# Sums of four heads in two packed attentions: one piece of eight products, or two halves in neighbouring steps

## The chip, the cores and the metric

The kernel runs on one core of a Trainium2 chip. The metric is the device time of one execution in microseconds. TensorE (PE in the profile) multiplies matrices, VectorE (DVE), ScalarE (ACT) and GpSimd (POOL) work element by element, and SyncE (SP) issues the transfers. Each engine works through its own list of instructions in order, and semaphores tie the lists together.

## What is computed

The reference is a chain of four attention layers on 16 sequences of 128 rows by 256 numbers. Layers 0 and 2 are ordinary transformer layers. Layers 1 and 3 are the ones that matter here: attentions with 16 heads of only 8 channels each, over 256 positions ("units" are its two halves of 128). Layer 1 needs for each head the mean and the spread of the values, layer 3 a plain attention. Cut to the core:

```python
# layer 1
attn = softmax(einsum('bhqd,bhdk->bhqk', q * scale, k))
mean = einsum('bhqk,bhkd->bhqd', attn, v)
ex2 = einsum('bhqk,bhkd->bhqd', attn, v * v)
std = sqrt(relu(ex2 - mean * mean))
# layer 3
attn = einsum('bhqd,bhkd->bhqk', Q, K) / math.sqrt(DH)
ctx = einsum('bhqk,bhkd->bhqd', softmax(attn), V)
y = ctx @ Wo
```

## The kernel before

The stages run one after the other: layer 0 to about 1270 us of the span, layer 1, layer 2 from about 1600 us, layer 3 from about 2184 us, and its feed-forward to the end. Both packed attentions are made by the same function, `attention(third, ...)`, with `third` 0 for layer 1 ("attention 1" from here on) and 1 for layer 3 ("attention 3"). A window is one batch, 16 windows run the core, and each window has 16 steps `j`, one for each head. The order of the instructions on every engine is written out by hand, step by step, and pieces of neighbouring batches are mixed into one window: `core` is batch n itself, `following` the next one, `carry` the one before, `ahead`, `coming` and `fourth` later ones.

In every step PE makes, for head j of this batch, two products of shifted scores (line 925) and, for head j of the next batch, two products of plain scores (line 934). Both use 32 rows of the array (form 32*128); the text calls the four a pair. DVE takes the maxima of the plain scores (line 1725), ACT the exponential of the shifted ones (line 1405) into `probs_t`. Shifted scores have two banks, so the pair of step j waits until the exponential of step j-2 is done.

Four heads make a pack. When the exponentials of a pack are there, PE sums them with the values (line 984): for each unit c and each of the four heads m one product of form 128*32, each with 32 columns of its own, all into `sum_bank`, half of bank 5. A product of plain floats appears as two instructions, so a pack is 16 instructions. They stand in steps 3, 7, 11 and 15; those of step 3 are the last pack of the batch before. ACT copies the bank out one step later (line 1362), at the head of its steps 0, 4, 8 and 12.

The other half of bank 5 is `spare`. PE turns the maxima there (line 905, steps 1 and 9), DVE copies them out at the head of its steps 2 and 10 (line 1706), and SP moves the copies into rows of q by four transfers (line 2331), which the shifted scores of steps 0 and 8 wait for. In attention 3 PE also turns the heads there (line 1053, step 13), ACT copies them (line 1389, step 14), and the output product (line 1061, step 15) takes that copy. As both halves are in one bank, the sums wait for each of these copies, and these turns wait for the copy of the sums.

Other pieces of a window: projections of q and k (lines 953 and 960; q in step 2, k in step 2 or 3), placing of q and k for later heads (line 912; in attention 1 in steps 0, 11 and 14, in attention 3 in steps 0, 1, 10 and 11; ACT and DVE copy them out, k for the first heads by line 1738), the turn of the summed heads (line 999, steps 6 and 7), the values (line 1010, step 9), in attention 1 the result (line 1022, step 12), whose copies by ACT (lines 1384 and 1385) free the bank that k's placing of step 14 takes. Attention 3 prepares later batches as well: DVE aggregates statistics in step 5 (line 1986), POOL makes the inverse roots from them (lines 2196 to 2202) and the normed rows (line 2206), and PE turns these in step 13 (line 1037), followed by the turn of the placed rows (line 1046). Where two pieces share a step, they stand in the order of the code, in which the sums come behind the scores, projections and the turn of maxima, and ahead of the placings of `place_q_first` and `place_k_first`, the turns of lines 999 to 1053 and the result.

```python
SCHEDULE1 = Schedule(place_k=0, project_k=2, turn=(6, 7), values=9, place_q_first=11, place_k_first=14, result=12)
SCHEDULE3 = Schedule(place_k=1, project_k=3, turn=(6, 7), values=9, place_q_first=11, place_k_first=10, result=15)
TURN_MAXIMA = (9, 1)
LAST_SUMS = 3
```

Of the kernel before, what the change touches and what calls it, by code (L numbers as in the profile page):

```python
# [29 lines left out]
D = 256  # L30
# [20 lines left out]
HN = 16  # L51
# [8 lines left out]
PACK = 4  # L60
# [162 lines left out]
LAST_SUMS = 3  # L223
STD_PARTS = 4
# [188 lines left out]
def program(nc, t, out, outer):  # L413
# [303 lines left out]
    def _(pe):  # L717
# [173 lines left out]
        def attention(third, w_q, source_q, w_k, w_v, when):  # L891
# [5 lines left out]
            def window(n, at, u=None):  # L897
# [18 lines left out]
                for j in range(HN):  # L916
# [51 lines left out]
                    if j % PACK == LAST_SUMS and (j > LAST_SUMS and core or j == LAST_SUMS and carry):  # L968

                        g = (j // PACK - 1) % PACKS  # L970
                        v = vn[u] if j > LAST_SUMS else vn[1 - u]
                        if g == 0:
                            pe.wait_ge(s.v_taken if third else s.v_ready, n + 1)
                        pe.wait_ge(s.exp_ready, HN * n + j - 3)
                        after(pe, s.sums_copied, PACKS * n + j // PACK - 1)
                        if j == LAST_SUMS:
                            pe.wait_ge(s.max_copied, 2 * n + (2 if core else 0))
                        if j == TURN_MAXIMA[0] + 2 and following:
                            pe.wait_ge(s.max_copied, 2 * (n + 1) + 1)
                        if j == HN - 1 and third and carry:  # L980
                            pe.wait_ge(s.heads_copied, i)
                        for c in range(UNITS):
                            for m in range(PACK):
                                last = pe.matmul(sum_bank[quad[m], :], v[:, c, PACK * g + m, :],  # L984
                                                 probs_t[(PACK * g + m) % 8][:, c * D:(c + 1) * D], start=c == 0, stop=c == UNITS - 1)
                        last.then_inc(s.sums, 1)
# [61 lines left out]
                    if third and carry and j == 13:  # L1048
                        pe.wait_ge(s.heads_taken, heads_taken(1, n))
                        if core:  # L1050
                            pe.wait_ge(s.sums_copied, PACKS * n + 2)
                        for unit in range(UNITS):
                            last = pe.transpose(spare[:, unit * P:(unit + 1) * P], heads_out[unit][:, 0:P], ident[:, :])
                        last.then_inc(s.heads_turned, 1)
# [175 lines left out]
    def _(act):  # L1230
# [107 lines left out]
        def attention(third, q_bias, k_bias, when):  # L1338
# [11 lines left out]
            def window(n, at, u=None):  # L1350
# [3 lines left out]
                for j in range(HN):  # L1354
# [32 lines left out]
                    if third and carry and j == 14:  # L1387
# [1030 lines left out]
```

## Time and profile before

| | us |
|---|---|
| median of 3 runs | 2591.17 (2588.92 to 2597.12) |
| the profiled execution, its own time | 2597.26 |
| its span, first to last instruction | 2595.5 |
| mean granted clock of TensorE | 0.932 of full |

PE is busy for 2261.8 us, DVE for 1783.5, ACT for 1481.9 and POOL for 718.5. Times in the timelines are microseconds from the start of the span: the start of a row, how long it lasts, the engine, the line, what is written and read, the shape, and how many neighbouring instructions the row merges. In brackets stands how long the engine was idle just before and what released it. A matmul's duration includes its way through the array, so neighbours overlap, and the distance between starts tells what one holds PE for. In a view of a narrow window only the instructions still running in it are merged.

### The profile page before, as it was taken

The page shows a single profiled execution, that of the slowest core. Times are in us where ns is not written, and L with a number is a line of the kernel's source. Part 1 is how long each engine was busy: PE and PEld are TensorE (multiplying, and loading weights), DVE is VectorE, ACT ScalarE, POOL GpSimd, SP SyncE. Part 2 cuts the span into 40 slices and gives each one's busy share as a digit, 9 for nine tenths or more (in the row PEclk, how much of TensorE's full clock was granted, in tenths as well). Part 3 has the DMA queues.
Part 4 walks back from the last instruction along what each step waited for, and adds up shares of the span by engine and source line. Part 5 has one row for each costly group of instructions (what it writes and reads, how often), then busy time and mean ns, then how long its engine had stood idle before and what let it go on. Part 6 is the DMA issues. An engine that isn't in the chain of part 4 may idle for free. (4 is left out here: it accounts for less than half of the span.)

```text
span 2595.5 us, 53248 instructions
## 1 busy us (share of the span) xinstructions
PE 2261.8 (87%) x17289; PEld 1802.1 (69%) x17289; DVE 1783.5 (69%) x4693; ACT 1481.9 (57%) x4021; POOL 718.5 (28%) x1041
## 2 busy tenths in 40 slices
PE   4999999995999999979788885899998787888896
PEld 3898989984989899969655553566665784555553
DVE  5666666667666666666577775888886654777746
ACT  2554545553555555557366765677777553666656
POOL 2111111111111111020245442666665104333200
PEclk7999999997999999989799997999999895999978
DMA  4100011000000100010000001000000000000000
GB/s 118 22 21 22 21 22 54 22 21 21 8 23 13 22 21 21 1 33 0 7 10 8 10 5 66 7 0 5 16 15 10 4 5 7 9 8 8 3 3 32
DMA packets 72941, 47.12 MB, mean 18 GB/s; under 512 B 29232, under 2 KB 71601, under 8 KB 72753
## 3 DMA queue, kind: packets, MB, share of 16 engines
q1 hardware_dynamic: 72752, 44.62, 6.5%
q8 instruction: 117, 1.92, 0.3%
q14 instruction: 72, 0.58, 0.1%
HBM read 41.45 MB, written 2.10 MB: 17 GB/s over the span
## 5 line engine op out<-in xcount | busy, mean ns | idle before, releaser
L1725 DVE TENSOR_REDUCE maxima<-bank 128x2 f32<-128x512 f32 x512 | 343.6, 684 | 176.3 <-PE bank L934 174.3
L1405 ACT ACTIVATE probs_t<-bank 128x512 f32<-128x512 f32 x512 | 292.0, 600 | 73.0 <-PE bank L925 68.3
L1281 ACT ACTIVATE wide_probs_t<-bank 128x256 f32<-128x256 f32 x256 | 98.5, 385 | 310.5 <-PE bank L814 308.3
L2047 POOL TENSOR_TENSOR wide_columns<-wide_pair_columns,zero 128x8 f32<-128x8 f32 x16 | 4.4, 278 | 861.4 <-DVE x L1622 816.5
L925 PE MATMUL bank<-q_packed,k_packed 32*128 32x256 f32 x1024 | 209.3, 351 | 31.3 <-ACT probs_t L1405 31.1
L1286 ACT ACTIVATE wide_probs<-bank,wide_neg_max 128x129 f32<-128x129 f32 x512 | 184.1, 365 | 84.7 <-DVE wide_neg_max L1592 80.4
L934 PE MATMUL bank<-k_packed,q_packed 32*128 32x256 f32 x1024 | 209.5, 352 | 8.3 <-DVE k_packed L1738 5.0
L1293 ACT ACTIVATE wide_heads_high<-bank,wide_columns 128x128 fp32r<-128x128 f32 x512 | 160.3, 365 | 96.6 <-PE bank L826 95.3
L925 PEld LDWEIGHTS bank<-q_packed,k_packed 32*128 32x128 f32 x1024 | 127.2, 200 | 120.7 <-ACT probs_t L1405 62.5
L1597 DVE RECIPROCAL wide_inverse<-wide_sums 128x2 f32<-128x2 f32 x256 | 42.5, 166 | 224.6 <-ACT wide_probs L1286 224.6
L1611 DVE SCALAR_TENSOR_TENSOR wide_heads_low<-bank,wide_columns,wide_heads_high 128x128 fp32r<-128x128 f32 x512 | 155.1, 344 | 40.9 <-ACT wide_heads_high L1293 35.5
L1599 DVE TENSOR_SCALAR wide_probs<-wide_probs,wide_inverse 128x128 f32<-128x128 f32 x512 | 172.3, 379 | 9.0
L1432 ACT ACTIVATE probs<-scores_masked,neg_max 128x128 f32<-128x128 f32 x512 | 163.2, 394 | 20.3 <-DVE neg_max L1907 18.7
L720 PE MATMUL bank<-wide_weights_high,wide_heads_high 128*128 128x256 f32 x512 | 166.1, 324 | 1.3 <-DVE wide_heads_low L1611 1.3
L826 PEld LDWEIGHTS bank<-wide_probs_t,wide_v 128*128 128x128 f32 x1024 | 149.3, 191 | 23.8 <-ACT wide_probs_t L1281 7.1
L804 PE MATMUL bank<-wide_k,wide_q 128*128 128x129 f32 x1024 | 156.4, 275 | 8.5 <-issue 8.5
L826 PE MATMUL bank<-wide_probs_t,wide_v 128*128 128x128 f32 x1024 | 157.2, 276 | 4.7 <-ACT wide_probs_t L1281 4.7
L984 PE MATMUL bank<-probs_t,vn 128*32 128x256 f32 x2048 | 155.0, 425 | 4.9 <-DVE max_rows L1706 3.4
L804 PEld LDWEIGHTS bank<-wide_k,wide_q 128*128 128x128 f32 x1024 | 140.2, 191 | 15.0 <-issue 9.3
L720 PE MATMUL bank<-wide_weights_high,wide_ctx_high 128*128 128x256 f32 x512 | 148.0, 289 | 0.0
L721 PE MATMUL bank<-wide_weights_low,wide_heads_high 128*128 128x256 f32 x512 | 144.2, 282 | 0.0
L722 PE MATMUL bank<-wide_weights_high,wide_heads_low 128*128 128x256 f32 x512 | 144.0, 281 | 0.0
(296 smaller groups left out, 6900.5 us busy)
## 6 DMA issues: line engine op xcount, KB each, us to landing
cn<-in_ctx SPq DMA_DIRECT2D x48, 128.0 KB, 2.0
wide_pair_weights<-in_L_xattn_wq SPq DMA_DIRECT2D x16, 256.0 KB, 2.9
wide_pair_weights<-in_L_xattn_wk SPq DMA_DIRECT2D x16, 256.0 KB, 3.3
wide_pair_weights<-in_L_xattn_wv SPq DMA_DIRECT2D x16, 256.0 KB, 3.8
wide_pair_weights<-in_L_xattn_wo SPq DMA_DIRECT2D x16, 256.0 KB, 3.6
q_packed<-max_rows SPq DMA_DIRECT2D x256, 4.0 KB
wide_ctx_rows<-in_ctx SPq DMA_DIRECT2D x4, 512.0 KB, 5.3
x<-in_x SPq DMA_DIRECT2D x4, 512.0 KB, 6.3
```

What stands on the lines that cost most here:

```text
L720: pe.matmul(acc, wh, mh, start=start, stop=False)
L804: last = pe.matmul(wide_scores[b % 2][:, h * KEYS0:(h + 1) * KEYS0], q0[k % 2][:, h, b * P:(b + 1) * P], k0[k % 2][:, h, b, :], start=True ...
L826: last = pe.matmul(wide_heads[a % 2][:, h * P:(h + 1) * P], v0[parity][:, a, h * P:(h + 1) * P], probs_t0[:, a, h, :], start=True, stop=True)
L925: last = pe.matmul(shifted_bank[j % 2][:, c * D:(c + 1) * D], k_packed[u][quad[a], pack, c * P:(c + 1) * P], q_packed[u][quad[a], pack, :] ...
L934: last = pe.matmul(head_scores[packed_scores(1 - u, j)][:, c * D:(c + 1) * D], q_packed[1 - u][quad[b], pack, c * P:(c + 1) * P], k_packed ...
L1286: last = act.activation(probs0[:, b, h, :], wide_scores[b % 2][:, h * KEYS0:(h + 1) * KEYS0], ACT.Exp, bias=neg_max0[:, b, h:h + 1], accum ...
L1293: last = act.activation(heads_high[:, h, a, :], wide_heads[a % 2][:, h * P:(h + 1) * P], ACT.Identity, bias=columns[slot][:, 3, h:h + 1])
L1405: act.activation(probs_t[j % 8][:, :], shifted_bank[j % 2][:, :], ACT.Exp, bias=0.0).then_inc(s.exp_ready, 1)
L1432: last = act.activation(probs[t][:, part], scores_masked[t][:, part], ACT.Exp, bias=neg_max[t][:, h:h + 1])
L1599: last = dve.tensor_scalar(probs0[:, b, h, 0:P], probs0[:, b, h, 0:P], inverse0[:, b, h:h + 1], None, ALU.mult)
L1611: last = dve.scalar_tensor_tensor(heads_low[:, h, a, :], wide_heads[a % 2][:, h * P:(h + 1) * P], columns[slot][:, 3, h:h + 1], heads_high ...
L1725: dve.tensor_reduce(maxima[pack // 2][:, b, pack % 2, :], head_scores[packed_scores(1 - u, j)][:, :].rearrange("p (a k) -> p a k", a=UNITS ...
```

## The change

The eight products of a pack are made in two halves, unit 0 in steps 2, 6, 10 and 14 and unit 1 in steps 3, 7, 11 and 15. All waits go to the first half; only the second raises the semaphore `sums`. The exponentials waited for are the same. The wait for DVE's copy of the turned maxima stands in steps 2 and 10, where it stood in 3 and 11. In attention 3 the turn of the heads moves from step 13 to 12, ACT's copy of it from step 14 to 13, and the wait for that copy from step 15 to 14. Nothing else moves.

```diff
--- before.py
+++ after.py
@@ -221,6 +221,7 @@
 PLACE_Q, PROJECT_Q = 0, 2
 TURN_MAXIMA = (9, 1)
 LAST_SUMS = 3
+SUMS = (2, 3)
 STD_PARTS = 4
 RSTD_STEPS = 2 + 3 * 4
 
@@ -965,25 +966,27 @@
                         if core:
                             pe.wait_ge(s.sums_copied, PACKS * n + 1)
                         turn_maxima(n + 1, 0)
-                    if j % PACK == LAST_SUMS and (j > LAST_SUMS and core or j == LAST_SUMS and carry):
+                    if j % PACK in SUMS and (j > LAST_SUMS and core or j <= LAST_SUMS and carry):
 
                         g = (j // PACK - 1) % PACKS
                         v = vn[u] if j > LAST_SUMS else vn[1 - u]
-                        if g == 0:
-                            pe.wait_ge(s.v_taken if third else s.v_ready, n + 1)
-                        pe.wait_ge(s.exp_ready, HN * n + j - 3)
-                        after(pe, s.sums_copied, PACKS * n + j // PACK - 1)
-                        if j == LAST_SUMS:
-                            pe.wait_ge(s.max_copied, 2 * n + (2 if core else 0))
-                        if j == TURN_MAXIMA[0] + 2 and following:
-                            pe.wait_ge(s.max_copied, 2 * (n + 1) + 1)
-                        if j == HN - 1 and third and carry:
-                            pe.wait_ge(s.heads_copied, i)
-                        for c in range(UNITS):
-                            for m in range(PACK):
-                                last = pe.matmul(sum_bank[quad[m], :], v[:, c, PACK * g + m, :],
-                                                 probs_t[(PACK * g + m) % 8][:, c * D:(c + 1) * D], start=c == 0, stop=c == UNITS - 1)
-                        last.then_inc(s.sums, 1)
+                        c = SUMS.index(j % PACK)
+                        if c == 0:
+                            if g == 0:
+                                pe.wait_ge(s.v_taken if third else s.v_ready, n + 1)
+                            pe.wait_ge(s.exp_ready, HN * n + PACK * (j // PACK))
+                            after(pe, s.sums_copied, PACKS * n + j // PACK - 1)
+                            if j < LAST_SUMS:
+                                pe.wait_ge(s.max_copied, 2 * n + (2 if core else 0))
+                            if j == TURN_MAXIMA[0] + 1 and following:
+                                pe.wait_ge(s.max_copied, 2 * (n + 1) + 1)
+                            if j == HN - 2 and third and carry:
+                                pe.wait_ge(s.heads_copied, i)
+                        for m in range(PACK):
+                            last = pe.matmul(sum_bank[quad[m], :], v[:, c, PACK * g + m, :],
+                                             probs_t[(PACK * g + m) % 8][:, c * D:(c + 1) * D], start=c == 0, stop=c == UNITS - 1)
+                        if c:
+                            last.then_inc(s.sums, 1)
                     for unit in range(UNITS):
                         if carry and j == when.turn[unit]:
 
@@ -1045,7 +1048,7 @@
                         for k in range(4):
                             last = pe.transpose(upper[:, k * P:(k + 1) * P], placed_packed[:, k // 2, k % 2 * P:(k % 2 + 1) * P], ident[:, :])
                         last.then_inc(s.turned, 1)
-                    if third and carry and j == 13:
+                    if third and carry and j == 12:
                         pe.wait_ge(s.heads_taken, heads_taken(1, n))
                         if core:
                             pe.wait_ge(s.sums_copied, PACKS * n + 2)
@@ -1384,7 +1387,7 @@
                         act.activation(mean_t[:, ds(at(-1), 1), :].rearrange("p a d -> p (a d)"), lower[:, 0:D], ACT.Copy)
                         act.activation(std_t[:, ds(at(-1), 1), :].rearrange("p a d -> p (a d)"), lower[:, D:2 * D], ACT.Relu)\
                            .then_inc(s.x_added, 1)
-                    if third and carry and j == 14:
+                    if third and carry and j == 13:
                         act.wait_ge(s.heads_turned, i)
                         act.activation(heads_t[0][:, :], spare[:, :], ACT.Copy).then_inc(s.heads_copied, 1)
                     if third and coming and j == 14:
```

## Rows read from the trace of the kernel before

**Rows 1.** The profile's page: busy time of the engines, granted clock in 40 slices

```profile
PE 2261.8 (87%) x17289; PEld 1802.1 (69%) x17289; DVE 1783.5 (69%) x4693; ACT 1481.9 (57%) x4021; POOL 718.5 (28%) x1041
...
PEclk7999999997999999989799997999999895999978
```

**Rows 2.** Stretches: length, busy time of each engine, granted clock, DMA share, GB/s

```profile
1438.33:1457.66 19.33, 16.83 (x174) 10.75 (x166) 15.18 (x37) 13.31 (x27) 9.64 (x20) 1.00 0.03 8
2348.39:2370.72 22.33, 19.00 (x177) 11.55 (x175) 15.29 (x41) 14.45 (x30) 7.41 (x21) 0.92 0.02 7
2370.72:2391.64 20.92, 17.55 (x176) 11.05 (x175) 15.29 (x40) 14.05 (x30) 7.42 (x21) 1.00 0.02 8
2461.00:2484.00 23.00, 22.33 (x130) 12.87 (x128) 9.66 (x22) 10.78 (x22) 0.00 (x0) 0.50 0.01 2
```

**Rows 3.** Timeline of attention 1, steps 3 to 6: start us, us, engine, line

```profile
1429.87 0.38 PE L925 MATMUL bank<-q_packed,k_packed 32*128 32x256 f32 x1
...
1430.31 1.07 PE L984 MATMUL bank<-probs_t,vn 128*32 128x256 f32 x16
...
1431.31 0.38 PE L925 MATMUL bank<-q_packed,k_packed 32*128 32x256 f32 x1
...
1431.44 0.39 ACT L1362 ACTIVATE sums_copy<-bank 128x256 f32<-128x256 f32 x1 [0.44 <-PE bank L984]
...
1432.73 0.38 PE L925 MATMUL bank<-q_packed,k_packed 32*128 32x256 f32 x1 [0.91 <-ACT probs_t L1405]
```

**Rows 4.** The same eight products in two narrower windows: sets still running

```profile
1430.55 0.83 PE L984 MATMUL bank<-probs_t,vn 128*32 128x256 f32 x12
...
1430.76 0.61 PE L984 MATMUL bank<-probs_t,vn 128*32 128x256 f32 x8
```

**Rows 5.** Timeline of attention 1: step 15, then steps 10 to 14

```profile
1426.17 0.49 PE L934 MATMUL bank<-k_packed,q_packed 32*128 32x256 f32 x2 [0.24 <-DVE k_packed L1738]
...
1438.02 0.38 PE L925 MATMUL bank<-q_packed,k_packed 32*128 32x256 f32 x1
...
1438.33 0.27 DVE L1706 CAST max_rows<-bank 32x128 fp32r<-32x128 f32 x1
...
1438.74 1.07 PE L984 MATMUL bank<-probs_t,vn 128*32 128x256 f32 x16 [0.20 <-DVE max_rows L1706]
...
1439.96 0.36 PE L912 MATMUL bank<-q_high,place 128*128 128x256 f32 x1
...
1441.84 0.38 PE L925 MATMUL bank<-q_packed,k_packed 32*128 32x256 f32 x2
...
1442.70 0.36 PE L912 MATMUL bank<-k_high,place 128*128 128x256 f32 x1 [0.28 <-ACT std_t L1385]
```

**Rows 6.** Timeline of attention 3, steps 13 to 15; then waits of L1037

```profile
2375.86 0.65 PE L1037 MATMUL bank<-ident,norm_packed 128*128 128x128 f32 x4 [2.31 <-POOL norm_packed L2206]
...
2376.78 0.38 PE L1053 MATMUL bank<-ident,heads_out 128*128 128x128 f32 x2
...
2377.09 0.38 PE L925 MATMUL bank<-q_packed,k_packed 32*128 32x256 f32 x1
...
2377.20 0.38 ACT L1389 ACTIVATE heads_t<-bank 128x256 f32<-128x256 f32 x1 [2.49 <-PE bank L1053]
...
2377.73 1.07 PE L984 MATMUL bank<-probs_t,vn 128*32 128x256 f32 x16
...
  POOL norm_packed L2206: 67.5, 23
```

**Rows 7.** Timeline of attention 3, steps 10 to 12

```profile
2370.26 0.38 PE L912 MATMUL bank<-k_high,place 128*128 128x256 f32 x1
...
2370.72 0.27 DVE L1706 CAST max_rows<-bank 32x128 fp32r<-32x128 f32 x1
...
2372.36 0.38 PE L912 MATMUL bank<-q_high,place 128*128 128x256 f32 x1
...
2372.57 3.15 POOL L2206 TENSOR_SCALAR norm_packed<-turned_packed,mean_var,rstd 128x128 f32<-128x128 f32 x4 [0.31 <-POOL rstd L2202]
```

## The prediction

> **What bounds the kernel now.** I read the page first: TensorE (PE) is busy for 87% of the span, more than any other engine, and its granted clock reads 9 tenths or more in nearly every slice inside the attentions, 7, 5 and 7 at their ends [rows 1]. The change lies in the two packed attentions, about 1284 to 1590 us and 2184 to 2532 us, so I went on to periods of one batch. In attention 1 one batch takes 19.33 us with PE busy for 16.83, DVE for 15.18 and ACT for 13.31, all at full clock; in attention 3 it takes 20.92 us with PE 17.55, and 22.33 us when the clock falls on the way [rows 2]. No engine is saturated: the three run in step through short waits, and a delay counts only if no wait stands behind it. Hence the timeline of one batch, read for what each PE instruction waited for.
>
> The prices, at full clock. A pair (shifted scores and scores of one head) holds PE for 0.44 us, 1429.87 to 1430.31; eight sum products (16 instructions) hold it for 1.00 us, 1430.31 to 1431.31 [rows 3]. Inside these 16 the sets of four start at 1430.31, 1430.55 and 1430.76 [rows 3, 4]. A fourth set, estimated 0.21 behind the third (1430.97), is followed by the next kind of product at 1431.31, so leaving the sums costs 0.34 us where a set costs 0.21. **A half of two sets therefore costs 0.24 + 0.34 = 0.58 us, not 0.50; two halves with other work between them cost 1.16, or 0.16 us more than one piece.** The extremes are nothing extra (1.00 in two halves) and a whole leave-and-enter again of 0.34.
> The Trainium skill, "TensorEngine Tiling (Array Packing)", section Key Properties, says that a change of tiling mode drains TensorE. It speaks against this change, which adds 128 changes from 128*32 to another form; the trace agrees in sign and gives about 0.13 to 0.16 us for each.
>
> **Part by part, attention 1.** The work is the same 2048 instructions; no DMA and no instruction of DVE, POOL or SP is added or moved, and SP's row moves still follow the same DVE copies.
> Steps 2 and 3: the first half comes behind the projections, so pair 3 starts 0.58 later and the second half ends 0.16 later. ACT's copy of the sums waits for that end (0.44 us idle, 1431.44), then come k_high and three exps, and PE's pair 6 at 1432.73 waited 0.91 us for one of those exps [rows 3]. So +0.16 goes through. The exponential of head 3 also starts 0.58 later, but ends at 1431.6, where ACT idled until the copy anyway: nothing.
> Steps 6 and 7: PE runs without a gap from pair 6 to pair 8; +0.16.
> Steps 10 and 11 cost most. Now pairs 10 and 11 go out together at 1438.02 and the sums wait for DVE's copy of the maxima (1438.33, 0.27 long), starting at 1438.74; PE is free at 1439.74, and q's placing waits for DVE until 1439.96 [rows 5]. After the change the wait for that copy stands in step 10, ahead of pair 11. So 1438.74 + 0.58 + 0.44 + 0.58 = 1440.34 against 1439.96: +0.38. Queued behind the waiting half are pair 11 and, behind that, q's placing; ACT and DVE wait for both.
> Step 14: k's placing waits for ACT's std_t until 1442.70, pair 14 leaves PE at about 1442.28, so the half fills a hole of 0.42: +0.16. Step 15: PE gets free 0.42 earlier, but scores 0 at 1426.17 wait for DVE's k_packed [rows 5], which comes behind the maximum of head 15: no gain.
> Sum 0.16 + 0.16 + 0.38 + 0.16 = 0.86 us a batch, built on an estimated start of the fourth set; with that set 0.22 behind the third, as likely, a split costs 0.14 and the sum is about 0.77. I take 0.75. Sixteen batches: **+12 us** (bounds 0.2 and 1.2 a batch: +3 to +19).
>
> **Attention 3.** Twelve batches hang on POOL: PE's L1037 in step 13 waits 2.31 us for norm_packed [rows 6], whose last part starts at 2372.57 and takes 3.15 us [rows 7]. That chain begins with DVE's aggregation in step 5. So only what lies between L1037 and step 5 counts.
> Steps 13 to 15: the turn of the heads (L1053, 2376.78 to 2377.09, 0.31 us) leaves the path and goes into the stall. But pairs 14 and 15 went together at 2377.09, the sums at 2377.73 [rows 6], so L1061 could go at 2377.73 + 1.00 = 2378.73. New: 2376.78 + 0.44 + 0.58 + 0.44 + 0.58 = 2378.82: +0.09. ACT's copy of the heads, now in step 13, is ready in the stall. Steps 2 and 3: +0.16 as above. Together 0.25, taken as 0.2; times twelve **+2 us**.
> Steps 6 to 12 cost more, but are covered. k's placing (2370.26) stands behind the new wait for the maxima copy, which ends at 2370.99; then half 0.58, placing 0.66, pair 0.44, half 0.58 bring q's placing from 2372.36 to 2373.3 [rows 7]. With 0.16 of steps 6 and 7, L1053 (0.31) and pairs 12 and 13 apart (0.44) that is 1.85 us against the 2.31 of the stall: zero, with 0.46 us to spare. Without the cover: up to 1.85 x 12 = 22 us.
> The last four batches have no such stall and partly run at half clock (the stretch 2461 to 2484, 0.50, PE busy 22.33 of 23.00) [rows 2]: about 1 us each, **+4 us**.
>
> **The clock.** The granted clock fell to its half level (1.2 of 2.4 GHz) at several places behind the 2.31 us stall; a period with such a fall takes 22.33 instead of 20.92 us [rows 2], and the distances of L1037 show four such periods of twelve. In attention 1, whose longest regular hole is 0.91 us [rows 3], the batches run at full clock [rows 2]. The change cuts the stall to about 0.5 us, so some of the four falls should go: between 0 and -5.6 us (4 x 1.41); I take **-4**.
>
> **The sum:** 12 + 2 + 4 - 4 = +14 us. The profiled execution took 2597.3 us (span 2595.5 and 1.8 around it), 6.1 above the median of three runs; it would be 2611. Against the median of 2591.2 that gives **2605 us**, 0.54% slower. About 0.3% (7.8 us) is what a measurement of this kernel can tell from no change.
>
> **The rivals.**
> 1. *Faster: the clock decides.* Place: the stall in front of L1037 and the half-clock stretch behind it. For: L1037 sat idle 67.5 us in all for POOL [rows 6], and most falls lie behind it. If the shorter stall keeps the clock at full, four periods win 1.41 and the stretch from 2461, in which two half periods took some 29 us instead of 21, wins about 8: -14 in all. With PE's extra at half of my price (+8) the result is about 2585. It decides once the falls are worth more than the extra PE time, that is below 0.45 us a batch. Against: the stretch begins when the work of future batches ends, which the change leaves. Chance 0.17.
> 2. *No difference.* If a half costs just 0.50 and only the lost togetherness of pairs 10 and 11 is left (1438.74 + 0.50 + 0.44 + 0.50 = 1440.18, +0.22 a batch, 3.5 us), the clock's share cancels it: 2588 to 2598. The rows on the sets speak against it [rows 4]. The same result comes if DVE's order gives PE the delay back somewhere in the 4.15 us a batch in which DVE is idle [rows 2]. Chance 0.22.
> 3. *Slower still: the cover of attention 3 fails.* 0.46 us is little; a pair later, or the heads' turn waiting for ACT's copy of the sums in step 12, and L1037 is late by 0.5 to 1 us in twelve batches: +6 to +12, to 2611 to 2619. Chance 0.15.
> My forecast has 0.46, from 2598 to 2613. Faster by over 0.3%: 0.16; within: 0.22; slower by over 0.3%: 0.62 (the forecast, rival 3, less the edges). Leaving out the far ends of rivals 1 and 3, the range is 2587 to 2617.
> That the change doesn't do what it says can be excluded by the diff: every pack has both halves under the same conditions, and only the second raises the semaphore.
>
> **What would show it.** In the profile after: L984 in groups of 8, each holding PE for about 0.58 us; the period of attention 1 at 20.0 to 20.2 us instead of 19.33; PE waiting for DVE's max_rows in front of the half of step 10, with q's placing about 0.6 us later in the batch; attention 3 at 21.1 in clean batches, the wait in front of L1037 down to 0.3 to 0.9 us, and ACT's heads_t no longer waiting for PE 2.49 us [rows 6]. Wrong would be: halves of 0.50; a period of attention 1 under 19.5; pair 11 not behind the first half; L1037 with its old wait; or a half-clock share in attention 3 that falls by more than 10 us.

## The result, and the profile after

The changed kernel takes 2732.62 us, median of four runs (2727.19 to 2739.58), against 2592.06 us for the kernel before (2588.92 to 2597.12): ratio 1.0542, interval 1.0512 to 1.0571. It is slower, as forecast, but by 140.6 us and not by 14, and far outside the range. The profiled execution took 2732.58 us, its span is 2730.9 us and its mean granted clock 0.877.

The page of the changed kernel, the lines that answer to [rows 1]:

```profile
PE 2430.6 (89%) x17289; PEld 1870.5 (68%) x17289; DVE 1805.0 (66%) x4693; ACT 1493.9 (55%) x4021; POOL 711.3 (26%) x1041
...
PEclk9999999979999999897755555599999896899988
```

The same 17289 instructions hold PE for 169 us more. The row of the clock says where: six slices in a row read 5, about 1365 to 1775 us, which is attention 1 and the work just behind it. Before, the slices of attention 1 read 7 at both ends and 9 between [rows 1].

The windows view, one row for a stretch: length, busy us and instructions of PE, PEld, DVE, ACT and POOL, granted clock, DMA share, GB/s. First the changed kernel: attention 1 from the first to the last copy of maxima, its clean batch and a batch at the low level, then the same stretch of attention 3 (from the third copy on) and its clean batch.

```profile
1277.40:1719.80 442.40, 416.08 (x2476) 237.12 (x2475) 241.14 (x542) 209.13 (x402) 137.82 (x280) 0.55 0.02 5
1327.12:1347.28 20.16, 17.88 (x170) 10.74 (x166) 15.43 (x38) 13.43 (x27) 9.71 (x20) 1.00 0.03 10
1357.30:1463.00 105.70, 101.00 (x567) 56.59 (x566) 54.62 (x122) 47.24 (x92) 29.50 (x60) 0.50 0.02 5
1420.00:1451.13 31.13, 29.79 (x170) 16.85 (x168) 16.11 (x38) 13.98 (x27) 9.42 (x19) 0.50 0.02 5
2339.10:2640.60 301.50, 271.78 (x2481) 158.16 (x2481) 221.79 (x540) 203.50 (x409) 91.17 (x246) 0.99 0.02 7
2510.33:2531.51 21.18, 19.07 (x174) 11.16 (x174) 15.71 (x40) 14.33 (x30) 7.38 (x20) 1.00 0.03 8
```

The kernel before, the same two stretches:

```profile
1279.10:1579.10 300.00, 259.94 (x2476) 164.92 (x2475) 230.52 (x542) 200.39 (x403) 139.72 (x280) 0.95 0.03 8
2198.50:2507.70 309.20, 267.31 (x2477) 164.49 (x2477) 216.21 (x539) 201.15 (x409) 91.75 (x247) 0.92 0.02 7
```

Attention 1 lost 142.4 us and attention 3 won 7.7; together that is the 135 us between the spans. In attention 1 the mean clock is 0.55. As it has two levels, 1.2 and 2.4 GHz, the time at half is 2 x (1 - 0.55) x 442 = 398 us, against 30 before. A batch at half clock takes 31.13 us, and PE is busy for 29.79 of it (96%): PE that had to wait before is now the bound itself. The two prices add up to the loss of attention 1 (an estimate from these rows): 368 us more at half clock do the work of 368 x 20.16 / 31.13 = 238 us, so the clock costs 130 us, and sixteen batches of 0.83 us more work (below) cost 13.

What the change did to the work at full clock stands in the one clean batch. Timeline of the changed kernel, step 0, steps 2 and 3, then 9 to 11, then step 0 of the next batch (L986 are the sums, L926 and L935 the pair):

```profile
1334.85 0.49 PE L935 MATMUL bank<-k_packed,q_packed 32*128 32x256 f32 x2 [0.66 <-DVE k_packed L1741]
...
1338.02 0.59 PE L961 MATMUL bank<-hidden,w_keys 128*128 128x256 f32 x2
1338.55 0.64 PE L986 MATMUL bank<-probs_t,vn 128*32 128x256 f32 x8
1339.12 0.38 PE L926 MATMUL bank<-q_packed,k_packed 32*128 32x256 f32 x1
...
1340.12 0.38 PE L926 MATMUL bank<-q_packed,k_packed 32*128 32x256 f32 x1
...
1347.28 0.27 DVE L1709 CAST max_rows<-bank 32x128 fp32r<-32x128 f32 x1
...
1347.69 0.64 PE L986 MATMUL bank<-probs_t,vn 128*32 128x256 f32 x8 [0.22 <-DVE max_rows L1709]
...
1348.70 0.64 PE L986 MATMUL bank<-probs_t,vn 128*32 128x256 f32 x8
1349.27 0.39 PE L913 MATMUL bank<-q_high,place 128*128 128x256 f32 x1
...
1355.09 0.49 PE L935 MATMUL bank<-k_packed,q_packed 32*128 32x256 f32 x2 [0.67 <-DVE k_packed L1741]
...
1356.88 0.28 PE L926 MATMUL bank<-q_packed,k_packed 32*128 32x256 f32 x1
...
1357.31 0.58 PE L926 MATMUL bank<-q_packed,k_packed 32*128 32x256 f32 x1
...
1357.68 0.41 PE L926 MATMUL bank<-q_packed,k_packed 32*128 32x256 f32 x1
```

In the kernel before, the projection that stands there is this row, and pair 4 follows at 1431.31 [rows 3]:

```profile
1429.35 0.59 PE L960 MATMUL bank<-hidden,w_keys 128*128 128x256 f32 x2
```

A half holds PE for 0.57 us (1338.55 to 1339.12; forecast 0.58). From the projection to pair 4 it is 2.10 us, 0.14 more than before. From the sums of step 10 to q's placing it is 1.58 us, 0.36 more than before [rows 5] (forecast 0.38). The batch takes 20.16 us against 19.33, so +0.83. Then comes what nobody priced: PE sits idle for 0.67 us ahead of step 0's scores, where it was 0.24 [rows 5], and 2.2 us later the products stand further apart (1357.31 to 1357.68 is 0.37, where the same two stood 0.22 apart before). The clock has fallen, and the row from 1357.30 to 1463.00 shows that it stays down for 106 us. One batch earlier the same idle time of 0.66 us (up to 1334.85) was followed by no fall: it makes a fall likely, not certain.

The work in attention 3 came out as forecast, its clock better than forecast. Its timeline, steps 12 and 13, and the waits of PE in it (what waited, for what: us in all, times, longest):

```profile
2429.20 0.44 PE L1056 MATMUL bank<-ident,heads_out 128*128 128x128 f32 x2
...
2430.39 0.65 PE L1040 MATMUL bank<-ident,norm_packed 128*128 128x128 f32 x4 [0.31 <-POOL norm_packed L2209]
```

```profile
PE bank L1040 <- POOL norm_packed L2209: 4.1, 12, 0.4
```

The stall of 2.31 us ahead of L1037 [rows 6] is down to 0.31 (now L1040), so the cover held. A clean batch takes 21.18 us, and the mean clock went up from 0.92 to 0.99: before, it fell eight times behind the start, seven times for a few us and once for 24 us [rows 2], now never. The time at half clock in this stretch went from 48 to 8 us, where the prediction had -4 us for four falls and named a drop by more than 10 us as a sign of being wrong.

### The profile page after: what moved, and what is told of

The parts are those of the page before. It is cut to its first block and busy times, and to the rows that moved or that the text cites. A ratio compares the mean times of both kernels' runs of the same rounds, so it can differ in the third digit from the quotient of the medians.

```text
span 2730.9 us, 53248 instructions
## 1 busy us (share of the span) xinstructions
PE 2430.6 (89%) x17289; PEld 1870.5 (68%) x17289; DVE 1805.0 (66%) x4693; ACT 1493.9 (55%) x4021; POOL 711.3 (26%) x1041
## 5 line engine op out<-in xcount | busy, mean ns | idle before, releaser
L1728 DVE TENSOR_REDUCE maxima<-bank 128x2 f32<-128x512 f32 x512 | 350.2, 688 | 298.0 <-PE bank L935 292.1
L926 PE MATMUL bank<-q_packed,k_packed 32*128 32x256 f32 x1024 | 272.9, 407 | 26.2 <-ACT probs_t L1408 26.1
L926 PEld LDWEIGHTS bank<-q_packed,k_packed 32*128 32x128 f32 x1024 | 167.8, 242 | 167.9 <-ACT probs_t L1408 86.2
L935 PE MATMUL bank<-k_packed,q_packed 32*128 32x256 f32 x1024 | 271.0, 409 | 6.9 <-DVE k_packed L1741 4.4
L1284 ACT ACTIVATE wide_probs_t<-bank 128x256 f32<-128x256 f32 x256 | 98.5, 385 | 311.4 <-PE bank L815 309.2
L986 PE MATMUL bank<-probs_t,vn 128*32 128x256 f32 x2048 | 218.0, 509 | 13.7 <-DVE max_rows L1709 13.0
L935 PEld LDWEIGHTS bank<-k_packed,q_packed 32*128 32x128 f32 x1024 | 166.9, 243 | 16.0 <-issue 8.2
```

What stands on the lines that cost most here:

```text
L926: last = pe.matmul(shifted_bank[j % 2][:, c * D:(c + 1) * D], k_packed[u][quad[a], pack, c * P:(c + 1) * P], q_packed[u][quad[a], pack, :] ...
L935: last = pe.matmul(head_scores[packed_scores(1 - u, j)][:, c * D:(c + 1) * D], q_packed[1 - u][quad[b], pack, c * P:(c + 1) * P], k_packed ...
L1728: dve.tensor_reduce(maxima[pack // 2][:, b, pack % 2, :], head_scores[packed_scores(1 - u, j)][:, :].rearrange("p (a k) -> p a k", a=UNITS ...
```

## The experiments

The expectations name the theories by letters. Mine at the start (A) was that splitting makes the clock fall, so that the loss is clock and not work. Against it stood that more PE work must cost more time (C, tested by e3) and that the place of the piece decides, in halves or whole (D, tested by e4). A fall is a change of the granted clock from full to half. Each attention begins with a stretch at half clock, its start, and falls are counted behind it; the length of a start is counted from the attention's first copy of maxima. All kernels but the changed one place each pack by a table; the rest of the code is that of the kernels shown. The first list is for attention 1, the second for attention 3, with one entry for each pack. Unit 0 of a pack is made in the first step of an entry, unit 1 in the second; (3, 3) is the old place, and a pack's waits stand with its unit 0. In e2, e4, h3 and all kernels named f or m the turn of the heads is back in step 13 and its copy in step 14:

```diff
-SUMS = (2, 3)
+PLACES = [[(2, 3)] * 4, [(2, 3)] * 4]
...
+                    pack_at = PLACES[third][j // PACK]
+                    for c in range(UNITS) if j % PACK in pack_at and (j > LAST_SUMS and core or j <= LAST_SUMS and carry) else ():
+                        if j % PACK != pack_at[c]:
+                            continue
```

The time at half clock is worked out from the windows rows as above; the falls were counted along the granted clock in the trace. Each ratio is against the kernel before, run beside it on the same chip. It is an estimate of its own and not the quotient of the two medians; the two differ most for f4 (1.0007 against 1.0037).

**First four: which attention, and more or less work.** The kernel before ran at 2585.78 us.

```diff
 e1_attention3
+PLACES = [[(3, 3)] * 4, [(2, 3)] * 4]
 e2_attention1
+PLACES = [[(2, 3)] * 4, [(3, 3)] * 4]
 e3_repeat (changed kernel; in attention 1 unit 0's products twice; first entry attention 1, [unit 0, unit 1])
+REPEATS = [[2, 1], [1, 1]]
...
+                        for r in range(REPEATS[third][c]):
 e4_whole_early (whole pieces in steps 2, 6, 10, 14 of attention 1; attention 3 as before)
+PLACES = [[(2, 2)] * 4, [(3, 3)] * 4]
```

> The two halves (and the earlier turn of the heads) in attention 3 alone; attention 1 has its whole pieces in steps 3, 7, 11 and 15. Theory A (attention 1 loses its granted clock, attention 3 is harmless): 2590 to 2600 us, attention 1 at 19.3 us a batch, attention 3 at 21.1 us with hardly a fall of the clock. Rival B (the halves cost PE time in both attentions alike, some 70 us each): about 2660 us.

> The two halves in attention 1 alone; attention 3 is as before. Theory A: 2725 to 2740 us, nearly the whole loss, with attention 1 at 31 us a batch at half clock. Rival B: about 2660 us.

> The changed kernel, with the first half of each pack of attention 1 made twice in a row (the first pass is overwritten by the second), 512 instructions more. Theory A (the array has too little to do at half clock for the clock to come back): the clock comes back and the time falls below the changed kernel's 2733, to about 2592 + 14 + 64 x 0.45 = 2635 us. Rival C (the clock is lost by something else, and more work is just more work): 64 x 0.84 us more at half clock, about 2785 us.

> Attention 1 with the whole piece of eight products in steps 2, 6, 10 and 14, with the waits of the change; attention 3 as before. Theory A (splitting loses the clock): the clock stays as before, and about 0.8 us a batch go into waits: 2595 to 2610 us. Rival D (the earlier waits, above all PE's wait for the maxima copy in step 10 ahead of pair 11, lose the clock): 2700 us or more, at half clock.

Measured: e1 2594.34 us, ratio 1.0019 (0.9993 to 1.0045); e2 2704.11 us (2654.54 to 2728.78; no ratio on record); e3 2641.24 us, 1.0199 (1.0159 to 1.0239); e4 2728.69 us, 1.0561 (1.0530 to 1.0591). Attention 1 in the windows views of e1, e2, e3 and e4:

```profile
1273.30:1573.40 300.10, 259.98 (x2476) 164.98 (x2475) 230.42 (x542) 200.36 (x403) 139.75 (x280) 0.95 0.03 8
```

```profile
1276.80:1716.60 439.80, 412.66 (x2477) 235.55 (x2477) 241.58 (x542) 209.43 (x403) 137.50 (x280) 0.56 0.02 5
```

```profile
1276.20:1646.90 370.70, 334.47 (x2950) 196.78 (x2948) 239.11 (x542) 203.69 (x403) 137.63 (x280) 0.85 0.02 7
```

```profile
1276.30:1711.00 434.70, 378.21 (x2478) 228.10 (x2476) 239.14 (x542) 202.62 (x403) 137.32 (x280) 0.63 0.02 5
```

The profiled executions of e2 (2728.78 us) and e3 (2671.57 us) are the slowest of their four, so their rows show more loss than the median. The loss comes from attention 1 (e1 has none of it, e2 118 of 141 us by the medians). e3 is the clearest: 512 instructions **more**, and 91 us less than the changed kernel, with the clock at 0.85 instead of 0.55. A had 2635 for it and C 2785: the loss is clock, not work. But e4 takes the halves away and keeps the loss, as D had it. So halves are not needed for it, and my first theory falls in that part; the place of the piece matters. e1's lack of a gain in attention 3 is its start, which ran at half clock for 87 us, against 22 in the kernel before and 31 in the changed one, whose attention 3 is the same; behind that it had no fall.

**Next four: which pack.** The kernel before ran at 2595.15 us.

```diff
 f1_steps10
+PLACES = [[(3, 3), (3, 3), (2, 3), (3, 3)], [(3, 3)] * 4]
 f2_all_but10
+PLACES = [[(2, 3), (2, 3), (3, 3), (2, 3)], [(3, 3)] * 4]
 f3_steps14
+PLACES = [[(3, 3), (3, 3), (3, 3), (2, 3)], [(3, 3)] * 4]
 f4_steps2_6
+PLACES = [[(2, 3), (2, 3), (3, 3), (3, 3)], [(3, 3)] * 4]
```

> Attention 1: only the pack of steps 10 and 11 in halves, the other three whole in steps 3, 7 and 15; attention 3 as before. Theory E (the new place of the wait for the maxima copy, ahead of pair 11, loses the clock): 2690 us or more, at half clock through attention 1. Rival F (each split adds to the time that the array runs thinly, no single one decides): 2588 + 16 x 0.38 = about 2594 us, clock mostly full.

> Attention 1: the packs of steps 2/3, 6/7 and 14/15 in halves, that of step 11 whole; attention 3 as before. Theory E: the clock holds, 2588 + 16 x 0.48 = 2594 to 2600 us. Rival F: three of four splits are enough to lose it in part or whole, 2650 to 2720 us.

> Attention 1: only the pack of steps 14 and 15 in halves; attention 3 as before. Theory E and rival F both: about 2588 + 16 x 0.15 = 2590 us. If this one loses the clock (2650 us or more), neither holds, and the hole that the half filled ahead of k's placing was what counted.

> Attention 1: the packs of steps 2/3 and 6/7 in halves; attention 3 as before. Theory E: about 2588 + 16 x 0.32 = 2593 us with the clock of before. Rival F: between that and f2, 2600 to 2700 us.

Measured: f1 2631.40 us, 1.0137 (1.0105 to 1.0169); f2 2650.69, 1.0209 (1.0176 to 1.0242); f3 2631.73, 1.0125 (1.0096 to 1.0154); f4 2604.79, 1.0007 (0.9978 to 1.0036). Attention 1 of f1, f2, f3, f4:

```profile
1275.10:1613.20 338.10, 302.13 (x2477) 186.25 (x2475) 232.28 (x541) 204.10 (x402) 139.25 (x280) 0.82 0.02 7
```

```profile
1277.10:1630.60 353.50, 315.12 (x2477) 185.86 (x2477) 234.38 (x542) 203.40 (x403) 138.56 (x280) 0.78 0.02 7
```

```profile
1274.90:1617.20 342.30, 301.71 (x2478) 185.15 (x2476) 231.29 (x541) 202.99 (x403) 139.21 (x280) 0.81 0.02 7
```

```profile
1277.70:1579.50 301.80, 264.54 (x2476) 163.93 (x2475) 231.87 (x541) 200.09 (x402) 139.34 (x280) 0.96 0.03 8
```

Splitting the packs of steps 2/3 and 6/7 costs 1.8 us of attention 1 and not one fall; a clean batch takes 19.62 us, 0.28 more than before, 0.14 for each split. Splitting the pack of steps 10/11 alone costs 38 us, the one of 14/15 alone 42 us. Neither E nor F had this: E had f1 at 2690 us and f2 and f3 at full clock, F had f1 and f3 at 2594 us or less.

In f1 there are five falls. Three stand 0.8 to 1.1 us behind the end of the wait of 0.22 us that PE has ahead of the first half of step 10; the other two stand behind pair 6's wait of 0.9 us for `probs_t` [rows 3], where both falls of the kernel before stand. Its start lasts 71 us, against 24 before. One of the three, with the second half already at half clock:

```profile
1355.58 0.64 PE L989 MATMUL bank<-probs_t,vn 128*32 128x256 f32 x8 [0.22 <-DVE max_rows L1712]
...
1356.69 1.08 PE L989 MATMUL bank<-probs_t,vn 128*32 128x256 f32 x8
```

In f3 there are twelve falls, nine of them within 3 us of the idle time ahead of step 0's scores, three behind pair 6's wait. f2, which splits the packs of f3 and f4 together and leaves that of step 11 whole, has nine falls, all behind that idle time, and loses 53.5 us in attention 1: the wait of step 10 isn't needed for a loss.

**Next four: the idle places, and the turn of the heads by itself.** The kernel before ran at 2597.76 us.

```diff
 h1_turn_early (all sums whole in their old steps; turn and copy of the heads one step earlier)
-                    if third and carry and j == 13:
+                    if third and carry and j == 12:
...
-                    if third and carry and j == 14:
+                    if third and carry and j == 13:
 h2_turn_repeated (h1, the turn five times)
-                        for unit in range(UNITS):
+                        for unit in 5 * (0, 1):
 h3_fill_step0 (f3, step 0's shifted scores twice)
-                        for c in range(UNITS):
+                        for c in (0, 1) if j or third or not following else (0, 1, 0, 1):
 h4_warm_start (e1, unit 0's sums twice in the first two windows of attention 3)
+                        repeats = 2 if c == 0 and third and isinstance(n, int) and i < 2 else 1
```

> The kernel before, with nothing of the change but the turn of the heads in step 12 and its copy in step 13 (attention 3); all sums whole. Theory G (the 2.3 us stall ahead of L1037 makes the clock fall, and its copy by ACT is off the path): 12 x 0.31 less, 2584 to 2590 us against 2588 to 2592 before, with some 10 falls left in attention 3, since the stall is still some 1.6 us. Rival: no difference at all.

> As h1, with the turn of the heads made five times over (the same result each time), so that it fills the stall ahead of L1037 with products. Theory G: the falls in attention 3 go from 9 to 0 to 3, and with them 4 to 6 times 1.4 us: 2578 to 2586 us. Rival H (it was the halves that kept the clock up in attention 3, not the shorter stall): falls as in h1, and no gain over it.

> As f3 (attention 1: only the pack of steps 14 and 15 in halves), with the shifted scores of step 0 of attention 1 made twice, which fills the hole ahead of the plain scores of step 0 (0.53 us there in f3, 0.24 before). Theory I (the hole of step 14 was moved to step 0 and joined the one there, and that longer hole makes the clock fall): the 12 falls of f3 go to 5 or fewer and the time from 2632 to 2590 to 2605 us. Rival J (the halves as such, shorter bursts of products, make it fall): 2625 to 2640 us as f3.

> As e1 (attention 3 in halves, attention 1 as before), with the first half made twice in the first windows of attention 3, up to its second batch. Theory K (at half clock the thinner products of the halves delay the clock's return; once up it stays up): the half-clock stretch at the start of attention 3 shrinks from 74 us to 10 to 30, and the time from 2594 to 2578 to 2588 us. Rival L (its length is chance): no difference from e1.

Measured: h1 2567.68 us, 0.9893 (0.9870 to 0.9916); h2 2577.76, 0.9925 (0.9904 to 0.9947); h3 2622.91, 1.0106 (1.0081 to 1.0130); h4 2589.82, 0.9963 (0.9948 to 0.9979). Attention 3 of h1, a row of its timeline, then attention 1 of h3:

```profile
2188.30:2478.40 290.10, 257.70 (x2481) 160.09 (x2481) 217.86 (x539) 202.24 (x409) 90.80 (x247) 0.99 0.02 7
```

```profile
2358.62 0.65 PE L1043 MATMUL bank<-ident,norm_packed 128*128 128x128 f32 x4 [1.44 <-POOL norm_packed L2212]
```

```profile
1274.70:1600.00 325.30, 288.14 (x2508) 179.50 (x2507) 230.83 (x542) 202.65 (x403) 139.29 (x280) 0.87 0.03 7
```

h1 is the part of the change that helps, and by more than either expectation had. The turn of the heads, and pair 13 that now goes apart from pair 12, fill 0.87 us of the stall (2.31 to 1.44 us), a clean batch goes from 20.92 to 20.45 us, and the falls behind the start of attention 3 go from eight to none in the profiled executions; 309.2 us became 290.1. More work in the stall (h2: 128 instructions more) brought nothing on top: no fall in either, and h2 is 10 us slower. h3 makes f3's idle time at step 0 smaller (0.67 to 0.44 us in most batches, 0.53 to 0.29 in the others); its attention 1 is 17 us shorter than f3's, with eight falls instead of twelve, more than the five that I had. The intervals of the two ratios overlap, so by itself this is a hint. h4 cut the start of attention 3 from e1's 87 us to 28 (h4's expectation counts e1's 74 us from a later copy), and its ratio is 0.6 points below e1's, the intervals apart.

**Three more: the idle place told apart from the halves.** What was still open on record: whether the loss comes from *where* PE is left idle (I) or from halves as such (J). The kernel before ran at 2586.28 us.

```diff
 m1_whole_in_14 (no halves anywhere)
+PLACES = [[(3, 3), (3, 3), (3, 3), (2, 2)], [(3, 3)] * 4]
 m3_whole_in_10 (no halves anywhere)
+PLACES = [[(3, 3), (3, 3), (2, 2), (3, 3)], [(3, 3)] * 4]
 m2_copy_earlier (f1; in attention 1 DVE copies the maxima before its work on head 9, not in step 10)
-                    if following and j == TURN_MAXIMA[0] + 1:
+                    if third and following and j == TURN_MAXIMA[0] + 1:
...
+                    if not third and following and j == TURN_MAXIMA[0]:
+                        copy_maxima(n + 1, 0)
                     own(n, at, u, j)
```

> Attention 1: the pack of step 15 whole, but in step 14; the others whole in 3, 7 and 11; attention 3 as before. No halves anywhere. Theory I (where PE is left with nothing to do counts, and taking the sums out of step 15 leaves it idle ahead of step 0's plain scores): at least as many falls of the clock as f3 (12), 2630 us or more. Rival J (halves as such lose the clock): 2 to 4 falls as before, 2590 to 2600 us.

> As f1 (attention 1: only the pack of steps 10 and 11 in halves), with DVE's copy of the maxima one piece earlier, ahead of its work on the heads of step 9, so that PE doesn't wait for it ahead of the first half. Theory I: fewer falls than in f1 (5, with 50 us at half clock behind the start), 2595 to 2610 us. Rival J: 2620 to 2635 us as f1.

> Attention 1: the pack of step 11 whole, but in step 10, ahead of pair 11; the others whole in 3, 7 and 15; attention 3 as before. Theory I: PE waits as in f1, but then has 1.0 us of products in one piece: 2600 to 2630 us, like f1 or a little better. Rival J: 2590 to 2600 us, the clock of before.

Measured: m1 2683.47 us, 1.0379 (1.0360 to 1.0399); m2 2616.70, 1.0116 (1.0099 to 1.0133); m3 2598.99, 1.0042 (1.0027 to 1.0058). Attention 1 of m1 and its waits of PE ahead of step 0's plain scores (L936), then a row of its timeline:

```profile
1276.60:1669.20 392.60, 341.12 (x2477) 206.88 (x2476) 237.86 (x541) 202.89 (x403) 139.00 (x280) 0.68 0.02 6
```

```profile
PE bank L936 <- DVE k_packed L1744: 13.3, 8, 1.7
...
PE bank L936 <- issue: 9.1, 6, 1.5
```

```profile
1622.35 0.47 PE L936 MATMUL bank<-k_packed,q_packed 32*128 32x256 f32 x2 [1.51 <-issue]
...
1622.97 0.41 PE L914 MATMUL bank<-q_low,place 128*128 128x256 f32 x1
1623.18 0.42 PE L914 MATMUL bank<-q_high,place 128*128 128x256 f32 x1
```

The same waits in f3, in h3, and in the kernel before:

```profile
PE bank L936 <- DVE k_packed L1744: 5.5, 8, 0.8
PE bank L936 <- issue: 3.2, 6, 0.5
```

```profile
PE bank L936 <- DVE k_packed L1744: 3.6, 8, 0.5
...
PE bank L936 <- issue: 1.7, 6, 0.3
```

```profile
PE bank L912 <- ACT std_t L1385: 3.6, 13, 0.3
...
PE bank L934 <- DVE k_packed L1738: 1.9, 8, 0.2
...
PE bank L934 <- issue: 0.3, 1, 0.3
```

Right behind the idle 1.51 us of m1 the products of the placing stand 0.21 apart (1622.97 to 1623.18): half clock. And the four kernels make a series. Idle ahead of step 0's scores, both releasers added: before 2.2 us, h3 5.3, f3 8.7, m1 22.4. Falls of the clock behind the start: 2, 8, 12, 18. Sorted by what PE did just before, these falls stand at two places only: within 3 us of the idle time ahead of step 0's scores 0, 4, 9 and 14, and behind pair 6's wait 2, 4, 3 and 4. The length of the idle time at step 0 decides how often a fall follows within 3 us. Counted where it is met at full clock: of 0.3 us and less none of 15 (before, h3), of 0.43 to 0.53 us six of 14 (h3, f3), of 0.67 to 0.77 us seven of eight (f3), of 1.5 to 1.7 us all 14 (m1). The idle time comes first and the fall second, so it isn't an effect of the fall.

m1 has not one half, and its ratio is 2.5 points above that of f3, which has them: for this place J falls and I stands. The way of it is plain in the waits. The pack stood in step 15, ahead of the scores that wait for DVE's k_packed. What is taken out of step 15 leaves its time as idle time at that wait; and in step 14 it fills a short hole (std_t, 3.6 us in thirteen pieces, no longer among the waits of f3 and m1). Several short holes are joined into one.

Attention 1 of m2 and m3:

```profile
1279.40:1601.70 322.30, 288.43 (x2476) 178.14 (x2475) 230.97 (x541) 203.01 (x402) 140.46 (x280) 0.87 0.03 7
```

```profile
1273.90:1584.30 310.40, 274.31 (x2476) 174.41 (x2475) 232.35 (x541) 198.80 (x402) 138.93 (x280) 0.92 0.03 8
```

m2 takes away the wait for the maxima copy that f1 has ahead of its first half. Behind the start its time at half clock is 16 us instead of 51, and attention 1 is 16 us shorter. Its first 71 us stay cold as in f1, and the ratios of the two overlap, so by the times the wait's part at step 10 is a hint. The place of the falls says more: the three that f1 has behind step 10 are gone, and the four of m2 all stand behind pair 6's wait, where f1 has two (a fifth comes only at the very end of the attention). With the pack whole in step 10 (m3), behind the same wait, there is one fall, also behind pair 6's wait, and the start lasts 47 us; its time, 2598.99 us, lies where J had it. So at step 10, other than at step 0, it takes the wait and the halves, which put pairs 10 and 11 apart. That rests on one profiled execution of each kernel.

**The last three: both cures in the changed kernel, and the best version.** The kernel before ran at 2596.82 us.

n1_cured is the changed kernel with these two lines, that of m2 (with its other edit) and that of h3; n2_turn_copy_early is h1 with the first of them; n3_turn_early_again is h1 once more:

```diff
+                    if not third and following and j == TURN_MAXIMA[0]:
+                        copy_maxima(n + 1, 0)
...
-                        for c in range(UNITS):
+                        for c in (0, 1) if j or third or not following else (0, 1, 0, 1):
```

> The changed kernel, whole, with the two cures in attention 1: DVE's maxima copy of step 9 made one piece earlier (as m2), and the shifted scores of step 0 made twice to fill the idle place there (as h3). Theory I (the idle places that the change leaves cost the clock, and the halves themselves little): far below the changed kernel's 2733, to 2640 to 2680 us, since h3's filling was partial. Rival (the four halves together keep the array thin enough to stay at half clock): 2710 us or more.

> All sums whole, the turn of the heads in step 12 (as h1), and in attention 1 DVE's maxima copy one piece earlier (as m2). Against h1 it takes a wait of 0.2 us a batch away from PE, behind which PE waits for DVE's values anyway: the same as h1 within 3 us, some 20 to 30 us faster than before.

> h1 once more, with more rounds: all sums whole, the turn of the heads in step 12 and its copy in step 13. 20 to 30 us faster than before, 1 fall of the clock or none in attention 3 behind its start.

Measured: n1 2669.24 us (2646.45 to 2705.48), 1.0286 (1.0251 to 1.0320); n2 2569.38, 0.9885 (0.9855 to 0.9915); n3 2568.54, 0.9898 (0.9875 to 0.9922). Attention 1 of n1, attention 3 of n2 and of n3:

```profile
1270.40:1637.00 366.60, 338.86 (x2506) 199.56 (x2505) 235.82 (x541) 205.25 (x402) 139.27 (x280) 0.74 0.02 6
```

```profile
2197.20:2495.40 298.20, 268.01 (x2477) 165.42 (x2477) 217.52 (x540) 203.29 (x409) 91.68 (x248) 0.94 0.02 7
```

```profile
2194.50:2484.70 290.20, 257.73 (x2481) 159.93 (x2481) 217.81 (x540) 202.25 (x409) 90.84 (x247) 0.99 0.02 7
```

The two cures give back half of the loss in the median (1.0286 against 1.0542), and 76 of the 142 us of attention 1 in the profiled execution, the fastest of the four. The other half is not traced. In part the cure of step 0 is incomplete: 0.44 us are left idle there in the first batches (0.67 in the changed kernel), and behind these 0.44 us the clock fell twice, once for 99 us. n3 confirms h1: sums whole, the heads' turn one step earlier, 1.0% **faster** than the kernel before. n2 shows that the falls vary: its profiled execution, the slowest of its four, has nine in attention 3, and the median is the same. So the turn takes the falls away in many executions, not in all.

## Why the prediction was wrong

**What held.** "A half of two sets therefore costs 0.24 + 0.34 = 0.58 us": 0.57. +0.16 in steps 2 and 3 and in 6 and 7: +0.14 each (also in f4). +0.38 in step 10: +0.36. The sum of 0.86 a batch: 0.83, where I had taken 0.75. Even the idle time ahead of step 0 is in the prediction's numbers: 0.24 was there, "PE gets free 0.42 earlier", which makes 0.66, and 0.67 was measured. I wrote "no gain" and left it there. Attention 3: 21.1 us forecast, 21.18 measured; the wait ahead of L1037 0.3 to 0.9 forecast, 0.31 measured; heads_t waits for PE no more. Rival 3, the lost cover, did not come. By themselves these steps give the forecast 12 us of attention 1 (16 x 0.83 = 13), and f4, which has two of the splits and no fall, is at 1.0007. That the kernel came out slower, as forecast, is still no merit of the mechanism: the forecast work is about a tenth of the 140.6 us.

The Trainium skill, "TensorEngine Tiling (Array Packing)", section Key Properties, says that a change of tiling mode drains TensorE. The trace agrees in sign, with 0.14 us more for a split; that draining is what takes this time is not shown.

**The step that failed** is the paragraph "The clock". It read "In attention 1, whose longest regular hole is 0.91 us, the batches run at full clock", priced the clock at 0 there, and at -4 us in attention 3 alone. The sentence is true of the kernel before, but for two short falls in attention 1, and the price of 0 does not follow. What stood in its place was 368 us more at half clock, about 130 us of time. Full clock was a state that attention 1 only just held. The change moved two pieces of idle time. It put a wait ahead of the half in step 10, and it turned the time of half a pack in step 15 into idle time ahead of step 0's scores (0.24 to 0.67 us). f1 and f3 show that the change at either place is enough for falls; m1 shows for step 0 that it is the idle time there, and the series of four that falls grow with it; e3 and e4 show that neither the amount of work nor the halves alone explain the loss. For step 10 the cause is narrowed to the half behind the wait with the pairs apart (f1 against m2 and m3), not settled. I had found both places (the wait "in step 10", the 0.42 us of step 15) and asked only what they cost in time on the path, never what they do to the clock.

**Rival 1** named the clock as what decides, with the other sign and the other attention. Its own place behaved as it said: all eight falls in attention 3 went, worth 7.7 us net of PE's extra time there, where the prediction's terms for attention 3 add up to +2. So the -4 for the clock there was mis-sized too: I counted four falls from the distances of L1037, where the granted clock has seven short ones and the one of 24 us. Of the 67.5 us for which L1037 waits [rows 6], 26.5 lie in attention 3. "It decides once the falls are worth more than the extra PE time" was the right question, and attention 1 answered it with +142 us. The range was made from the bounds of a sum at full clock; it had no case in which the clock of a whole attention is lost, so it could not hold the time.

**What stays open.** How the falls of attention 1 add up: the two idle places alone give 38 and 42 us, all four packs 142. Once the clock is down, PE is busy for 96% of the time with short gaps, and it still stays down for 89 to 219 us at a time in the changed kernel (99 us in n1), while the short falls of the kernel before end after a few us. Twice it came back in the changed kernel, and both times it fell again 0.4 us behind the wait of 0.22 us ahead of the half of step 10. Why starts last 71 us when pairs 10 and 11 are apart (f1, m2) was not told apart either, nor why that of attention 3 lasts 87 us in e1 and e3 and 31 us in the changed kernel and n1, which split it in the same way. Where the first halves are doubled the starts are short: 25 us in attention 1 (e3) and 28 in attention 3 (h4).

## What to carry to other kernels

Before a piece of TensorE work is moved, ask what is left idle where it stood, and whether that joins a wait: in f3, half a pack taken out of step 15 cost attention 1 42 us through the granted clock, where its extra work was priced at 2.6 (16 x 0.16). Where a kernel runs at full clock with a few short falls, count the clock as a term of its own with a wide bound in both directions, and read it per stage (duration, PE busy, clock), since a high busy share looks the same at either level. Move the pieces one by one: here the small one, the turn of the heads into a stall, gives -1.0% alone, and beside the halves nobody would have seen it.

## What was not expected of the hardware

- A busy engine that stays at half clock: from 1357 us the changed kernel ran at half clock for 106 us with PE busy for 101.0 of 105.7 us. The page "TensorE: Matmul & The Clock Gate" of the Trainium skill, section "A second HAM failure mode: psum-queue depth-cycling", says that in one kernel short idle times between groups of matmuls made the clock go to and fro between its levels. The traces agree as to the kind (the idle 0.67 and 1.51 us ahead of step 0's scores are mostly followed by falls); they show besides long stays at the low level.
- More work was faster: e3 makes 512 instructions more than the changed kernel and takes 2641.24 us against its 2732.62.
- At half clock a half piece holds PE for 1.02 us against 0.57 at full. Timeline of the changed kernel:

```profile
1422.30 1.08 PE L986 MATMUL bank<-probs_t,vn 128*32 128x256 f32 x8
1423.32 0.58 PE L926 MATMUL bank<-q_packed,k_packed 32*128 32x256 f32 x1
```
